# Setup and the first layer of a four-layer kernel in one block, with a semaphore for each group of loads

## The reference

```python
xn = _layernorm(x, axis=-1)
# s: 8 heads of 64; q, k, v = xn @ Wq, Wk, Wv; segments of 32 rows
sq = elu(q_s) + 1.0
att_mem = sq @ mem / (sq @ z)                       # memory of earlier segments
att_dot = softmax(q_s @ k_s.T * scale, axis=-1)     # within the segment
att = gate * att_mem + (1.0 - gate) * (att_dot @ v_s)   # gate = sigmoid(betas)
# f: ternary weights
gamma = mean(abs(W)) + 1e-6
Wt = sign(W / gamma) * minimum(round(abs(W / gamma)), 1.0)   # for W_fc and W_proj
h = layernorm(gelu(xn @ Wt_fc.T), ln_w, ln_b)
f = h @ Wt_proj.T
```

## Time and profile before

| quantity | value |
|---|---|
| median of three runs | 2918.56 us |
| profiled execution, its own time | 2920.24 us |
| span of the profiled execution | 2918.5 us |
| mean granted TensorE clock | 0.861 of full speed |
| busy: PE, DVE, ACT, POOL | 2498.9, 2313.0, 1688.5, 360.1 us |
| SP's first DMA issue begins | 0.81 us |
| SP's last DMA issue of the setup ends | 61.22 us |
| layer 0's first statistics on DVE | 64.03 us |
| layer 0's loop begins on DVE | 91.42 us |
| layer 0's last instruction on DVE ends | 515.5 us |

### The profile page before, as it was taken

One profiled execution on the slowest core, in us unless ns is written; L12 is line 12 of the kernel. 1 busy time (PEld: TensorE's weight loads), 2 busy tenths in 40 slices (PEclk: granted clock), 3 DMA queues, 4 the chain that ended last, 5 costly groups with the idle time before them and its releaser, 6 DMA issues. The chain is left out here.

```text
span 2918.5 us, 55784 instructions
## 1 busy us (share of the span) xinstructions
PE 2498.9 (86%) x18940; PEld 1894.7 (65%) x18940; DVE 2313.0 (79%) x6039; ACT 1688.5 (58%) x3432; POOL 360.1 (12%) x400
## 2 busy tenths in 40 slices
PE   1899999899999999876858988888898888898886
PEld 0566666677777777665836665666665666666565
DVE  1899999787878888676277888888888888888887
ACT  0677777565665665544355656565565655565654
POOL 0000000000000000024411111111111111111111
PEclk9999999899999999989968877678877778877777
DMA  9000000000000000020224433434443334443344
GB/s 241 6 0 0 0 0 0 1 2 1 0 1 0 1 0 1 3 83 17 67 76 99 110 96 78 87 96 112 99 103 81 86 86 111 99 109 85 83 92 112
DMA packets 94200, 169.63 MB, mean 58 GB/s; under 512 B 19240, under 2 KB 53296, under 8 KB 94000
## 3 DMA queue, kind: packets, MB, share of 16 engines
q0 software_dynamic: 25088, 67.14, 12.3%
q1 hardware_dynamic: 65600, 98.77, 11.0%
q10 hardware_dynamic: 3312, 1.32, 0.2%
HBM read 92.61 MB, written 11.67 MB: 36 GB/s over the span
## 5 line engine op out<-in xcount | busy, mean ns | idle before, releaser
L1141 ACT ACTIVATE b_neg<-b_neg,b_nmax 128x128 f32<-128x128 f32 (+1 forms) x512 | 191.1, 444 | 207.3 <-DVE b_nmax L1295 207.3
L2558 ACT ACTIVATE d_probs<-l_bank,w_b 128x256 f32<-128x256 f32 x512 | 210.8, 469 | 155.6 <-PE l_bank L2397 153.3
L2812 DVE TENSOR_TENSOR_SCAN d_state<-w,d_state 128x1024 f32<-128x1024 f32 x128 | 291.0, 2284 | 3.8 <-issue 3.4
L2397 PE MATMUL l_bank<-xnT,w_w 128*128 128x256 f32 x1024 | 245.1, 382 | 14.7 <-ACT d_probs L2558 14.7
L2408 PE MATMUL l_bank<-w_w,d_probs 128*128 128x128 f32 x2048 | 252.7, 276 | 0.0
L2408 PEld LDWEIGHTS l_bank<-w_w,d_probs 128*128 128x128 f32 x2048 | 244.9, 192 | 11.7 <-ACT d_probs L2558 5.3
L2338 PE MATMUL l_bank<-w 9*128 9x256 f32 x1040 | 214.6, 669 | 23.5 <-ACT w L2482 18.9
L94 POOL TENSOR_TENSOR ln_rstd<-ln_var_eps,minus_half 128x2 f32<-128x2 f32 x51 | 70.6, 1385 | 1236.2 <-DVE ln_var_eps L88 1236.2
L2521 ACT ACTIVATE w<-d_delta,w_A_log 128x255 f32<-128x255 f32 x520 | 220.2, 499 | 0.0
L2397 PEld LDWEIGHTS l_bank<-xnT,w_w 128*128 128x128 f32 x1024 | 184.7, 190 | 41.4 <-ACT d_probs L2558 21.6
L2338 PEld LDWEIGHTS l_bank<-w 9*128 9x128 f32 x1040 | 127.8, 320 | 95.7 <-issue 38.3
(11 more groups left out here) (406 smaller groups left out, 5709.4 us busy)
## 6 DMA issues: line engine op xcount, KB each, us to landing
d_bct<-l_bc SPq DMA_DIRECT2D x132, 512.0 KB, 4.1
d_state<-d_state POOLq DMA_DIRECT2D x96, 512.0 KB, 6.5
d_state<-d_state POOLq DMA_DIRECT2D x32, 256.0 KB, 4.1
d_state<-d_state POOLq DMA_DIRECT2D x32, 128.0 KB, 3.1
x_sorted<-x SPq DMA_DIRECT2D x1, 2580.0 KB, 26.8
y_rows<-x SPq DMA_DIRECT2D x1, 2112.0 KB, 26.7
c2e_xg<-x_sorted SPq DMA_DIRECT2D x16, 129.0 KB
w<-in_L_ffn_w_dram SPq DMA_DIRECT2D x1, 2048.0 KB, 10.6
```

The lines of the kernel that those rows point to most:

```text
L1141: done = nc.scalar.activation(neg[:, slot, cols], neg[:, slot, cols], ACT.Exp, bias=nmax[:, slot, a:a + 1], scale=-1.0)
L2397: done = nc.tensor.matmul(bank[:, b, i * T:(i + 1) * T], w.w1[:, e, k * P:(k + 1) * P], x1T[:, :], start=True, stop=True)
L2558: done = v.activation(hid[:, e % 2, k, :], bank[:, b, i * T:(i + 1) * T], ACT.Gelu, bias=w.b1[:, e, k:k + 1])
L2812: done = v.tensor_tensor_scan(group, dA[i][:, g % (NG - 1), :, :].rearrange("p m t -> p (m t)"), group, 0.0, ALU.mult, ALU.add)
```

## The change

The setup block goes away: `setup` now only allocates. Its instructions move into layer 0's block, in this order for each engine.

- SP: the first 4 tiles of `x` (256 KB) with a semaphore of their own, then `wq0`, `wk0` (`qk_loaded`), `wv0`, `wo0` (`vo_loaded`), the other 28 tiles of `x` (`x_loaded`), and then the same 28 loads and two writes of zeros as before.
- ACT: five DMAs (gate, raw W_fc, raw W_proj, `lnw0`, `lnb0`), the sigmoid, and then the prologue. A wait for `lnw0` and `lnb0` stands ahead of the loop.
- POOL: the constants, the first power, then the clearing of `probsT` (it was DVE's), then the second power.
- DVE: the statistics and the norm of sequence 0 as soon as the first 4 tiles of `x` are there; the ternary work is put between the steps of the prologue; waits for the constants, the rest of `x` and `probsT` ahead of the first `mask_memory`.
- PE: the product with ones after the first of the four projections, the eight pairs of transpositions after the last; `ternary_copied` is waited for ahead of the memory scores.

The raw weights lie in the tile `hT`, the ones in `th`, the comparison in `h`; the PSUM banks are those of layer 0 (`OUT`, `MEM`, `MEM + 1`). The fifteen semaphores of the setup are now the layer's, and are cleared with it.

```diff
-        @block.sync
-        def _(sp):
-            sp.dma_start(wfc[:, :, :], A["L0_ffn_W_fc"].rearrange("(c p) d -> p c d", p=P)).then_inc(c.w0_loaded, 16)
-            sp.dma_start(wproj[:, :], A["L0_ffn_W_proj"]).then_inc(c.w0_loaded, 16)
...
-        @block.vector
-        def _(dve):
-            nc.vector.memset(ones[:, :], 1.0)
-            dve.wait_ge(c.w0_loaded, 16 * 8)
...
+        @block.sync
+        def _(sp):
+            A = c.A
+            x_rows = A["L0_attn_x"].rearrange("b (a p) d -> p (b a) d", p=P)
+            early = 2 * TILES
+            sp.dma_start(c.x[:, 0:early, :], x_rows[:, 0:early, :]).then_inc(x_first, 16)
+            sp.dma_start(c.wq0[:, :], A["L0_attn_Wq"]).then_inc(qk_loaded, 16)
+            sp.dma_start(c.wk0[:, :], A["L0_attn_Wk"]).then_inc(qk_loaded, 16)
+            sp.dma_start(c.wv0[:, :], A["L0_attn_Wv"]).then_inc(vo_loaded, 16)
+            sp.dma_start(c.wo0[:, :, :], A["L0_attn_Wo"].rearrange("(c p) d -> p c d", p=P)).then_inc(vo_loaded, 16)
+            sp.dma_start(c.x[:, early:TILES * NSEQ, :], x_rows[:, early:, :]).then_inc(x_loaded, 16)
...
+            pe.wait_ge(consts_made, 1)
             turn_x(0)
-            for j in range(NCH0):
+            pe.wait_ge(qk_loaded, 16 * 2)
+            project_qk(0, 0, 0)
+            pe.wait_ge(abs_sums, 1)
+            nc.tensor.matmul(bank[:, OUT, 0:2], ones, abs_sum[:, :], start=True, stop=True).then_inc(totals, 1)
+            for j in range(1, NCH0):
                 project_qk(0, 0, j)
+            pe.wait_ge(ternary, 1)
+            for j in range(KF):
+                cols = slice(j * P, (j + 1) * P)
+                nc.tensor.transpose(bank[:, MEM, cols], raw_fc[:, j, :], c.ident[:, :])
+                done = nc.tensor.transpose(bank[:, MEM + 1, cols], raw_proj[:, cols], c.ident[:, :])
+            done.then_inc(ternary_turned, 1)
             for half in range(2):
                 denominators(0, half)
+            pe.wait_ge(vo_loaded, 16 * 2)
             for a in range(TILES):
                 project_v(0, 0, a)
+            pe.wait_ge(ternary_copied, 1)
             memory_scores(0, 0, 0)
...
+            act.dma_start(c.gate[:, :], betas[0].partition_broadcast(P)).then_inc(gate_ready, 16)
+            act.dma_start(raw_fc, c.A["L0_ffn_W_fc"].rearrange("(c p) d -> p c d", p=P)).then_inc(ff_loaded, 16)
+            act.dma_start(raw_proj, c.A["L0_ffn_W_proj"]).then_inc(ff_loaded, 16)
...
+            act.wait_ge(gate_ready, 16)
+            v.activation(c.gate[:, :], c.gate[:, :], ACT.Sigmoid).then_inc(gate_ready, 1)
             load_exp_ln(nc)
             copy_xnT(0, 0)
...
             load_gelu_tanh(nc)
+            act.wait_ge(ln_loaded, 16 * 2)
...
             norm_power(nc, c, s, 0)
+            nc.gpsimd.memset(probsT[:, :, :, :].rearrange("p o g k -> p (o g k)"), 0.0)
+            nc.gpsimd.drain().then_inc(probs_zeroed, 1)
             norm_power(nc, c, s, 1)
...
+            def ternary_limits():
+                dve.wait_ge(ff_loaded, 16 * 2)
+                v.tensor_reduce(abs_sum[:, 0:1], raw[0], AX, ALU.add, apply_absolute_value=True)
+                v.tensor_reduce(abs_sum[:, 1:2], raw[1], AX, ALU.add, apply_absolute_value=True).then_inc(abs_sums, 1)
+                dve.wait_ge(totals, 1)
+                v.tensor_scalar(limit[:, 2:4], bank[:, OUT, 0:2], 1.0 / (F0 * D), 1e-6, ALU.mult, ALU.add)
...
+                for i in range(2):
+                    v.tensor_scalar(below[:, i, :], raw[i], limit[:, 2 + i:3 + i], None, ALU.is_lt)
+
+            def ternary_values():
+                v.drain()
+                for i in range(2):
+                    done = v.scalar_tensor_tensor(out=raw[i], in0=raw[i], scalar=limit[:, i:i + 1], in1=below[:, i, :],
+                                                  op0=ALU.is_gt, op1=ALU.subtract)
+                done.then_inc(ternary, 1)
+                dve.wait_ge(gate_ready, 17)
+                v.tensor_scalar(c.gate1m[:, :], c.gate[:, :], -1.0, 1.0, ALU.mult, ALU.add)
+
+            def take_ternary():
+                dve.wait_ge(ternary_turned, 1)
+                v.tensor_copy(c.wfcT[:, :], bank[:, MEM, :])
+                v.tensor_copy(c.wprojT[:, :, :].rearrange("p c d -> p (c d)"), bank[:, MEM + 1, :])\
+                    .then_inc(ternary_copied, 1)
+
-            v.memset(probsT[:, :, :, :].rearrange("p o g k -> p (o g k)"), 0.0)
+            v.memset(ones, 1.0)
...
-            dve.wait_ge(c.x_loaded, 16)
+            dve.wait_ge(x_first, 16)
             norm_stats(nc, c, s, 0)
             norm_apply(nc, c, s, 0, True)
-            for half in range(2):
-                for i in range(2):
-                    elu_plus_1(0, 0, 2 * half + i)
-                times_z(0, 0, half)
-            for half in range(2):
-                share_q(0, 0, half)
+            ternary_limits()
+            elu_plus_1(0, 0, 0)
+            ternary_values()
+            elu_plus_1(0, 0, 1)
+            times_z(0, 0, 0)
+            for i in range(2):
+                elu_plus_1(0, 0, 2 + i)
+            times_z(0, 0, 1)
+            share_q(0, 0, 0)
+            take_ternary()
+            share_q(0, 0, 1)
             for a in range(TILES):
                 take_v(0, 0, a)
+            dve.wait_ge(consts_made, 1)
+            dve.wait_ge(x_loaded, 16)
+            dve.wait_ge(probs_zeroed, 1)
             mask_memory(0, 0)
```

More of the change, by code:

```diff
@@ L439, in layer0 @@
         u = sb("u", [P, TILES, D])
+        raw_fc, raw_proj = hT[:, 0, :, :], hT[:, 1, :, :].rearrange("p k d -> p (k d)")
+        ones, below = th[:, 0, :], h
+        abs_sum, limit = sb("abs_sum", [P, 2]), sb("limit", [P, 4])
+        x_first = sem("x_first_loaded")
+        x_loaded = sem("x_loaded")
+        ff_loaded = sem("ff_loaded")
+        qk_loaded = sem("qk_loaded")
+        vo_loaded = sem("vo_loaded")
+        ln_loaded = sem("ln_loaded")
+        zeros_made = sem("zeros_made")
+        consts_made = sem("consts_made")
+        gate_ready = sem("gate_ready")
+        abs_sums = sem("abs_sums")
+        totals = sem("totals")
+        ternary = sem("ternary")
+        ternary_turned = sem("ternary_turned")
+        ternary_copied = sem("ternary_copied")
+        probs_zeroed = sem("probs_zeroed")
         s = NormSems(sem, "n")
@@ L661, in exponentials @@
                     v.activation(rows, rows, ACT.Exp, scale=DK0 ** -0.5).then_inc(exp_ready, 1)
+            betas = c.A["L0_attn_betas"].rearrange("a h b v -> (a b) (h v)")
+            act.dma_start(c.gate[:, :], betas[0].partition_broadcast(P)).then_inc(gate_ready, 16)
+            act.dma_start(raw_fc, c.A["L0_ffn_W_fc"].rearrange("(c p) d -> p c d", p=P)).then_inc(ff_loaded, 16)
+            act.dma_start(raw_proj, c.A["L0_ffn_W_proj"]).then_inc(ff_loaded, 16)
+            with nc.allow_non_contiguous_dma("two small columns"):
+                act.dma_start(c.lnw0[:, :], c.A["L0_ffn_ln_w"].rearrange("(c p) -> p c", p=P)).then_inc(ln_loaded, 16)
+                act.dma_start(c.lnb0[:, :], c.A["L0_ffn_ln_b"].rearrange("(c p) -> p c", p=P)).then_inc(ln_loaded, 16)
+            act.wait_ge(gate_ready, 16)
+            v.activation(c.gate[:, :], c.gate[:, :], ACT.Sigmoid).then_inc(gate_ready, 1)
             load_exp_ln(nc)
@@ L799, in turn_probs @@
                 return done
-            v.memset(probsT[:, :, :, :].rearrange("p o g k -> p (o g k)"), 0.0)
+            raw = (raw_fc.rearrange("p c d -> p (c d)"), raw_proj)
+            def ternary_limits():
[5 more added lines that the diff above has]
+                v.drain()
+                v.tensor_scalar(limit[:, 0:2], limit[:, 2:4], 0.5, None, ALU.mult)
+                v.tensor_scalar(limit[:, 2:4], limit[:, 2:4], -0.5, None, ALU.mult)
+                v.drain()
+                for i in range(2):
+                    v.tensor_scalar(below[:, i, :], raw[i], limit[:, 2 + i:3 + i], None, ALU.is_lt)
+            def ternary_values():
+                v.drain()
+                for i in range(2):
[10 more added lines that the diff above has]
+            v.memset(ones, 1.0)
             v.memset(zsum[:, :, 0:1], 1.0 / DK0)
```

161 lines of the change are left out of this document (47 added, 114 removed).

## The result

The changed kernel took 2870.28 us (median of 4 runs, 2868.86 to 2870.80) against 2918.26 for the kernel before in the same series (2916.53 to 2919.69). The ratio is 0.9831, with a 95% interval of 0.9819 to 0.9843: 48.0 us faster. The forecast was 2861 with a range of 2854 to 2870: the setup block no longer holds the layer back, as forecast, but the gain is 9 us smaller than the sum made it, and the measured median lies at the range's upper end, 0.3 us above 2870.

A forecast was written before the change was run, and what follows sets the result against it. Bound at the start by SP's list of issues closing setup; loop at 9.4 + 23.69 + 0.8 = 33.9 us instead of 91.42, 57.5 earlier. 2920.24 - 57.5 = 2862.7, median 1.7 below: 2861 us, range 2854 to 2870.

The forecast's parts named there:

- The sum's frame: Setup and layer 0's start: SP's list of issues ends the setup block; without it the loop begins 57.5 us earlier.
- When the prologue can start: Layer 0's prologue: first projection at 9.4 us instead of 67.73, once wq, wk and raw weights land; 58.3 us earlier.
- POOL's clearing against L103: Rival, prologue: POOL's clearing of probsT holds up DVE's application of the norm, up to 1.8 to 2.2 us; chance 0.25.
- What the ternary work adds: Prologue, first projection to loop: ternary work between the steps delays the loop by a net 0.8 us.
- late-loads rival: Prologue: raw weights, wq and wk land at 12 to 15 us instead of 9.4, costing 2.6 to 5.6; chance 0.14.
- Traffic beneath compute: Engines beside full DMA engines: no slowing, taken as 0 us; 2% on 60 us would be 1.2.
- The gain given back later: Rival, layer 3: the earlier start and other code addresses shift its iterations, up to 10 us either way; chance 0.10.
- the clock: Rival, loop's first iterations: PE stays at 1.2 GHz, some 24 us more on each, 2933 us or more; chance 0.02.
- the change without effect: Rival, setup block: something other than SP's list ended it, so nothing moves, 2918 us; chance 0.01.

The follow-up runs named there:

- The early clearing: Changed kernel with POOL clearing probsT ahead of its first power instead of behind it: 2871.69 us, ratio 0.9823 to the kernel before.
- the changed kernel's other trace: The changed kernel, unedited, run again on one chip with three others: 2871.74 us, ratio 0.9835 to the kernel before.
- the zeros late: Changed kernel with SP waiting for sequence 9's norm before its two writes of zeros: 2867.59 us; repeated on one chip, 2866.86 us.
- all three edits: Changed kernel with zeros written late, probsT cleared before the first power, raw weights on SP's queue: 2864.98 us; repeated on one chip, 2863.50 us.

## Why the prediction was right or wrong

**The sum's frame held.** SP's list of issues was the end of the setup block; with it inside the layer nothing waits for it. From the second sequence to the layer's end both kernels agree to 0.2 us, and the fifteen semaphores and the barrier cost nothing that can be seen. SP's last issue ends at 66.38 us, not at the forecast 61, inside the layer and with nobody waiting for it.

**When the prologue can start: mis-sized by 3.3 us.** Predicted 9.4 for the first projection, measured 12.67. Of this 1.95 us is x's landing, which I had taken from wfc in the old queue without counting the raw weights on ACT's queue beside it; with them behind it on SP's own queue 1.33 of them come back, and the cause of the other 0.6 stays open. 1.27 us is POOL's clearing against L103. That was a rival with a chance of 0.25 and a price of 1.8 to 2.2; it happened, at 1.27: the pair ended 0.15 us after the clearing did (11.30 against 11.15) and would have ended at 10.03. The early clearing shows that this is the whole of it. The rule of the Trainium skill (SBUF — State Buffer, section Who interferes with whom) had it right, and these traces agree with it, 1.87 us beside the clearing against 0.60 alone; I should have counted it, since the order on POOL's queue puts the clearing in the very moment at which DVE is released.

**What the ternary work adds: as forecast, and better by luck in the first trace.** Predicted +0.8 us on the 23.69 us from first projection to loop, 24.5; measured 36.49 - 12.67 = 23.82. DVE's delay is there (first elu + 1 at t + 3.9, the second at t + 6.4 instead of 5.65). What made up for it is PE's clock, which the forecast had not counted on: the granted clock stayed at 1.00 over the four value products, 1.88 us. In the changed kernel's other trace it was at 0.50 over part of them, they took 2.77 us, and the stretch took 24.67. Over the ten traces of the changed kernel and its edits it is 23.8 to 25.1 us, the first trace's being the shortest. The copies lie in the idle time as forecast, of which 0.76 us is left.

**The late-loads rival** came true in a small way: wk landed at 1.87 + 8.7 = 10.6 us, the second raw weight at 10.1, but behind L103's delay nobody waited for them. x's rest was there long before 27.6.

**Traffic beneath compute: right for instructions, wrong for code.** I looked for slower instructions, found none, and took 0. That step failed: what is late under the traffic is a packet of instructions, and PE stands until 2.5 to 2.9 us after it. The rows that the step was read from could not show this: in the kernel before the zeros had landed by 75.3 us (48.55 + 26.7), and the first instruction packet after the start is at 86.3. It cost 6.9 us in the first sequence of the profiled execution (4.6 of idleness; PE reaches the group 0.9 later than with the zeros late, and the rest is its lower clock behind the stall) and 4.9 in the medians with the zeros moved away. At the barrier after layer 0 the trace is 9.7 us behind the forecast (468.0 against 515.8 - 57.5): 2.6 us are the loop's late start, 36.49 against 33.9, and 6.9 are this. With all three edits the gain is 55.8 us, against 57.5 forecast.

**The gain given back later, the clock, the change without effect:** the later layers give no more and no less than their usual scatter, the granted clock was 0.85 over the changed kernel's first sequence, 0.96 over it with the zeros late, and 1.00 from 80 us on, and the change does what it says.

What is argued, not shown: that the packet on q8 is PE's code. The profile does not name the engine of an instruction packet. The evidence is the distance of 2.5 to 2.9 us in eight stalls, the packet's lateness where the DMA engines are full, and that both go with the traffic when it is moved. Nor was it shown why the packet starts late (whether it queues behind the kernel's packets or is asked for later), or tried whether larger pieces for the zeros would hold the packet up less.

## What to carry to other kernels

A block that both computes and issues DMAs for later ends with its slowest list: look at SP's last issue before anything else, and put issues that nobody needs soon into the block that follows. When dense traffic is moved beneath a loop, look for packets of instructions in the loop's first turn; here the traffic was free from the second turn on, and cost 4.9 us in the first. A clearing that fills idle time on GpSimd belongs ahead of the one that another engine waits for, not right behind it.

## What the runs showed of the hardware that was not expected

- An idle time marked "issue" of 1.7 to 4.8 us in the middle of a group of equal matmuls appeared in eight cases, all with full DMA engines, each ending 2.5 to 2.9 us after the start of a 16 KB packet on the instruction queue; it is read here as a wait for code.
- PE's granted clock can fall to 0.50 behind such a stall and make it dearer: 4.61 us of idleness cost 6.9 us of the sequence.
- The same 4.8 MB of small writes slow nothing (26.3 and 26.6 us for each sequence, to 0.02) beneath a loop that has been run through once; no instruction packet was seen in the changed kernel's layer 0 after 92.8 us.
- A GpSimd clearing of 1.80 us that starts 0.08 us before a VectorE pair of `tensor_scalar` stretches the pair from 0.60 to 1.87 us.
- A second queue is not neutral: two loads of 256 KB on ACT's queue, moved behind the first loads of SP's own queue, let the first of SP's loads be used 1.3 us earlier (6.22 instead of 7.55 us).
